# A mixture-of-experts block: how each expert tile gets its tokens and gate weights, when the expert outputs are fetched, and where the late sums stand

## The reference

```python
logits = flat_x @ Wr                                  # 4096 tokens, 8 experts
top_vals, top_idx = jax.lax.top_k(logits, 2)
rw = softmax(top_vals)                                # two weights per token
g = einsum('nc,ech->neh', flat_x, Wg)                 # C = 128, HIDDEN = 512
u = einsum('nc,ech->neh', flat_x, Wu)
h = silu(g) * u
eo = einsum('neh,ehc->nec', h, Wd) * DEPTH_SCALE
out = sum over the two chosen experts of rw * eo
x = x + attn_a(norm(x)); x = x + ffn(norm(x)); x = x + attn_b(norm(x)); x = x + ffn(norm(x))
```

## Time and profile before

| | us |
|---|---|
| median of three runs | 1116.42 (1113.54 to 1125.42) |
| profiled execution | 1122.49 |
| its span, first to last instruction | 1120.4 |
| PE / PEld busy in it | 1004.0 / 710.5 |
| DVE / ACT / POOL busy in it | 749.3 / 675.4 / 543.2 |

### The profile page before, as it was taken

How to read it: one execution, slowest core, us unless ns; L and a number is a source line. 1 busy time by engine, 2 the same in 40 slices (tenths; PEclk the granted TensorE clock), 3 DMA queues, 4 the chain that set the end, 5 groups by cost and what they waited for, 6 DMA issues and landing times.

```text
span 1120.4 us, 28587 instructions
## 1 busy us (share of the span) xinstructions
PE 1004.0 (90%) x9290; PEld 710.5 (63%) x9290; DVE 749.3 (67%) x2249; ACT 675.4 (60%) x1399; POOL 543.2 (48%) x764
## 2 busy tenths in 40 slices
PE   2999999999989999999798889999888899999990
PEld 1354555554568999999534444445544789999990
DVE  4697889877777333356778889998888753334542
ACT  2376777755644545555377779999778445455550
POOL 3143447634632710357776656588337155005465
PEclk9998999987989999999768889999889899999995
DMA  5444566534145977887743333343221578778973
GB/s 152 114 107 110 146 160 167 133 106 95 43 128 181 286 233 238 259 266 233 170 104 84 88 92 88 91 114 88 74 52 55 164 231 253 228 236 266 272 226 113
DMA packets 201721, 175.02 MB, mean 156 GB/s; under 512 B 19812, under 2 KB 160616, under 8 KB 201576
## 3 DMA queue, kind: packets, MB, share of 16 engines
q1 hardware_dynamic: 193384, 156.41, 50.6%
q0 software_dynamic: 8192, 16.79, 5.1%
HBM read 122.99 MB, written 50.14 MB: 155 GB/s over the span
## 4 chain that ended last, share of the span: by engine, by line
PE 61%; DVE 14%; SPq 8%; issue 6%; DMA 6%; POOL 3%; ACT 1%; POOLq 0%; DVEq 0%; ACTq 0%
PE psS L358 10%; PE psO L324 8%; PE psS L1399 7%; PE psT L1406 7%; DVE mx L664 5%; PE psS L389 4%; PE psN L1422 3%; PE psO L1422 3%; PE psM L279 3%; PE psN L331 3%; PE psT L366 2%; PE psM L429 2%; SPq L1476 2%; SPq L1471 2%; DMA xin<-xg 1%
## 5 line engine op out<-in xcount | busy, mean ns | idle before, releaser
L664 DVE TENSOR_REDUCE mx<-psS 128x3 f32<-128x384 f32 (+1 forms) x512 | 309.9, 618 | 88.7 <-PE psS L389 50.4
L358 PE MATMUL psS<-kst,qst 48*128 48x256 bf16 (+1 forms) x1024 | 195.8, 281 | 38.1 <-DVE mx L664 26.7
L561 ACT ACTIVATE pT<-psT,scb 128x512 f32<-128x512 f32 x256 | 192.5, 772 | 48.1 <-PE psT L366 46.0
L366 PE MATMUL psT<-qst,kst 50*128 50x256 bf16 (+1 forms) x1024 | 191.9, 274 | 4.1 <-DMA qst<-scr_m 1.8
L1463 DVE TENSOR_TENSOR hT<-sg,psT 128x512 f32<-128x512 f32 x142 | 97.5, 687 | 142.1 <-PE psT L1406 118.6
L1282 POOL DMA_INDIRECT xg<-xn,slot x128 | 123.2, 963 | 118.8 <-DVE ysb L1458 71.0
L1399 PE MATMUL psS<-xTt,wgc 128*128 128x128 f32 x1136 | 153.3, 278 | 3.7 <-issue 3.5
L556 ACT ACTIVATE pT<-psT 128x384 f32<-128x384 f32 x256 | 123.5, 489 | 54.8 <-PE psT L366 46.7
L1406 PE MATMUL psT<-xTt,wuc 128*128 128x128 f32 x1136 | 151.6, 277 | 1.1 <-DMA wuc<-in_L_ffn_Wu 1.1
L358 PEld LDWEIGHTS psS<-kst,qst 48*128 48x128 bf16 x1024 | 63.5, 96 | 138.1 <-DVE mx L664 71.6
L1296 POOL DMA_INDIRECT pT<-eo,slot x64 | 60.6, 947 | 175.3 <-DVE ysb L1458 105.5
(11 more groups left out here) (230 smaller groups left out, 1601.0 us busy)
## 6 DMA issues: line engine op xcount, KB each, us to landing
wgc<-in_L_ffn_Wg SPq DMA_DIRECT2D x142, 256.0 KB
wuc<-in_L_ffn_Wu SPq DMA_DIRECT2D x142, 256.0 KB
scr_part<-part SPq DMA_DIRECT2D x128, 128.0 KB, 2.1
qst<-scr_part SPq DMA_DIRECT2D x64, 192.0 KB, 3.7
kst<-scr_part SPq DMA_DIRECT2D x64, 192.0 KB, 4.6
xin<-xg SPq DMA_DIRECT2D x142, 64.0 KB
eo<-ysb SPq DMA_DIRECT2D x142, 64.0 KB
scr_part<-part SPq DMA_DIRECT2D x32, 192.0 KB, 1.9
```

The lines of the kernel that those rows point to most:

```text
L358: return nc.tensor.matmul(ps[:, c0:c0 + n], q_[r64, t, q0], k_[r64, t, 0:n], start=(half == 0), stop=True, skip_group_check=True)
L366: return nc.tensor.matmul(ps[:, c0:c0 + T - q0], k_[m64, t, half * P:half * P + P], q_[m64, t, q0:T], start=(half == 0 or not L.causal), s ...
L561: nc.scalar.activation(pT[:, g % 8, 0:cols], psT[g % 2][:, 0:cols], ACT.Exp, scale=scb[r][:, 0, i:i + 1], bias=scb[r][:, 1, i:i + 1]).then ...
L664: nc.vector.tensor_reduce(mx3[:, u, 0:n, pos:pos + 1].rearrange("p a b -> p (a b)"), psS[h % 2][:, 0:kcols(L)].rearrange("p (a k) -> p a k ...
```

## The change

1. **Tokens without PE and PSUM.** `xin` is now loaded in pairs of tiles (`tiles_of`: tile 0 alone, then 1 and 2, 3 and 4, ...) by four DMAs, one for each 32 features. Each lays 32x32 blocks side by side, in rows of 32 floats, which are 128 bytes. DVE transposes all blocks with one instruction per pair (`dve_columns`), straight into `xTt`. PE's transpose and ACT's copy are gone, and with them the waits for the PSUM bank `psM`.
2. **Gate weights resident.** `wg` (128 x 4096) is loaded in attention A, steps 4 to 11. `act_gate` copies the gate weights of tile k + 2 from it; SP's gate loads are gone.
3. **SP's order.** The up weights of tile k + 2 stand ahead of the token load, and the wait for the second group's scatters stands behind them.
4. **Fetches in three parts.** The second group's blocks are split at 9 and 13 (`PARTS`) instead of at 11: they need the tiles up to 57, 65 and 71. The tables cost a further comparison and table stage 8 is divided over k = 6 to 9. POOL's first-group fetches of the second expert stage are paced by `pair // 2` instead of `2 * pair // 3`. The last quad is added in two pieces (blocks 12; 13 to 15) and stored apart.
5. **Sums in halves.** In attention B the sums stand at heads 3 and 5 (step 6: 3 and 7) of steps 3, 4, 6 and 7, four additions each; POOL's fetches all stand at the end of its step. Some routing work of attention A moves by one or two heads.

```diff
-PART = 11
+PARTS = (9, 13)
-        xin = [sb(f"xin{i}", [P, D]) for i in range(FETCH)]
-        xTt = [sb(f"xTt{i}", [P, P]) for i in range(FETCH)]
+        xin = [sb(f"xin{i}", [P, 2 * D]) for i in range(2)]
+        xTt = [sb(f"xTt{i}", [P, 2 * P]) for i in range(2)]
...
             if k == ROUTE_LN:
                 dve.wait_ge((LA, LB)[l].s["x1"], NBLK)
+                dve_columns(dve, l, 0)
                 dve_ln_stats(dve, NBLK - 4, NBLK, s_ln[n])
+                dve_columns(dve, l, 1)
                 dve.wait_ge(s_ln[n], 2)
...
-            for pair in range(2 * PART if l == 1 else 0):
-                pool.wait_ge(f_sem["y"], n0 + TILES - 4 * PART // 3 + 2 * pair // 3)
+            for pair in range(2 * PARTS[1] if l == 1 else 0):
+                pool.wait_ge(f_sem["y"], n0 + OWN_A)
...
+        def act_gate(act, l, t):
...
+            chosen[n] = expert(act, l, t)
+            after(act, f_sem["g"], n - FETCH + 1)
+            nc.scalar.activation(wgc[n % FETCH][:], wg[:, bass.ds(chosen[n], HID)], ACT.Copy
+                                 ).then_inc(f_sem["wg"], 1)
...
+        def dve_columns(dve, l, m):
+
+            i, width = m % 2, P * len(tiles_of(m))
+            after(dve, f_ld[i], 64 * (PAIRS // 2 * l + m // 2 + 1))
+            after(dve, f_sem["u"], l * TILES + max(2 * m - 3, 0))
+            nc.vector.transpose(xTt[i][:, 0:width], xin[i][:, 0:width]).then_inc(f_sem["xT"], 1)
...
+        def sp_load(sp, l, m):
+
+            tiles = tiles_of(m)
+            rows = xg[tiles[0] * P:(tiles[-1] + 1) * P, :].rearrange("(t b) (f a) -> f b t a", b=SQ, a=SQ)
+            after(sp, f_sem["xT"], PAIRS * l + m - 1)
+            for f in range(D // SQ):
+                sp.dma_start(xin[m % 2][SQ * f:SQ * f + SQ, 0:P * len(tiles)].rearrange("b (t a) -> b t a", a=SQ),
+                             rows[f]).then_inc(f_ld[m % 2], 16)
...
-                if l == 1 and (j, h) in ((4, 9), (5, 9), (7, 2), (8, 4)):
-                    dve_combine_1(dve, 0, (4, 5, 7, 8).index(j))
+                if l == 1 and j in SUMS_AT and h in (3, 7 if j == 6 else 5):
+                    dve_combine_half(dve, 0, SUMS_AT.index(j), int(h > 3))
```

More of the change, by code:

```diff
@@ L1518, in sp_ffn @@
                     sp.wait_ge(r_gat[q], 16 * 8 * l)
-            for t in range(3):
-                sp_load(sp, l, t)
+            for m in range(2):
+                sp_load(sp, l, m)
             for k in range(TILES + 3):
@@ L1940, in _ @@
             pool_ffn(pool, 1)
-            for pair in range(2 * PART, 2 * SIZE[1]):
+            for pair in range(2 * PARTS[1], 2 * SIZE[1]):
                 pool_gather(pool, 3, pair)
```

245 lines of the change are left out of this document (128 added, 117 removed).

## The result

| | before | changed |
|---|---|---|
| median, us | 1114.98 (4 runs, 1113.12 to 1125.42) | 1102.70 (4 runs, 1096.30 to 1108.33) |
| ratio to before | 1 | 0.9876, 95% interval 0.9831 to 0.9921 |
| profiled execution / its span | 1122.49 / 1120.4 | 1101.90 / 1099.4 |
| 0 to tile 0 of expert stage 1 | 328.2 | 326.4 |
| stage 1, tile 0 to tile 70 | 209.7 | 210.8 |

The change gives 12 us by the medians and 21 between the two profiled spans; the forecast was 39.6. The 1102.7 lies just inside the stated range, 1062 to 1104, at the end where rival 2 stood and far from the forecast's 1077. The tail did what was forecast.

A forecast was written before the change was run, and what follows sets the result against it. It took PE to set the expert stages' pace at 2.79 us per tile, with DMA the second bound. Terms of -15.4 + 4.8 - 4.4 - 2.8 - 11 - 10.8 = -39.6 took 1116.4 to 1077 us; range 1062 to 1104.

The forecast's parts named there:

- rival 2: Expert stages: SP becomes the bound, token issues taking 0.8 us each, 2.86 us a tile, 1102 us; 6 in 100.
- SP as a cover: Expert stages: SP's issues take 4.5 us of a pair's 5.36, so they stay hidden behind PE.
- the other terms: Everything in the sum except PE's transpose: stage starts, routing, tile 23, attention B's sums and tail, together -24 us.
- PE's transpose, -15.4: Expert stages: without PE's transpose a tile takes 2.68 us, 0.11 less over 140 tile distances, -15.4 us.
- The covers ACT, DVE, DMA: Expert stages: per 2.68 us tile, ACT's 1.82 plus 0.4, DVE's 1.9 at most and DMA's 1.89 us stay hidden.
- Rival 1: Expert stages: small token packets make DMA the bound, at 78 ns each some 1230 us; 9 in 100.
- The start of the stages, +4.8: Start of both expert stages: DVE waits for four token loads before its norm statistics, +4.8 us, from +2 to +9.
- Routing, -4.4: Expert stages: spreading the expert table over four tiles removes tile 7's stall, 2.2 us each stage, -4.4, from -7 to 0.
- Tile 23, -2.8: Both expert stages: weights no longer stand behind the wait for the scatters, -2.8 us, from -5 to +1.
- Sums, -11: Attention B: sums in halves cut steps 4 to 8 from 104.1 to 93 us, -11, from -16 to 0.
- Rival 3: Attention B: halved sums don't help, PE still idles or they meet POOL; term 0, time 1088 us; 15 in 100.
- Tail, -10.8: After tile 70: POOL's second-group fetches start earlier and the last sum is a block shorter, -10.8 us, from -7 to -13.

The follow-up runs named there:

- b_act_store: The kernel before, with none of the change, but the tiles' result stores issued by ACT instead of SP: 1109.42 us, 0.9938 of before.
- as_sp_dummy: The changed kernel with stores issued by ACT, plus one unneeded 512-byte transfer per tile in SP's queue in their old place: 1100.20 us, 0.9864 of before.
- The single run: The changed kernel with stores issued by ACT and one part undone: attention B's sums (1090.52 us) or, for the tail, the first fetch part's end at block 11 (1097.84).

## Why the prediction was wrong, step by step

- **SP as a cover: the step that failed.** The prediction counted a pair at 4.5 us of 5.36, with two table reads "which I count as plain", 0.42 each. A read with the register instructions behind it takes 0.75 us (425.79 to 426.53), and the pair 5.13. The four token issues were priced right, 1.91 us for 1.96. So the margin was 0.2 us per pair, not 0.86, and the prediction had no term for irregular issues. The 18 long issues add 0.24 us to the average pair, so that SP needs as long as PE. Not every slow issue became a stall: after the one at 430.48 PE kept its pace. Together they and the missing room cost 15 to 16 us of the stages (409.6 and 410.5 us, against 394.3 with the stores on ACT) and 23 of the medians.
- **Rival 2 was the right one in its place.** It said that SP becomes the bound and the kernel takes 1102, and it was given 6 in 100. Its condition, 0.8 us per token issue and so an even 2.86 us per tile, was wrong: issues take 0.48 us on average, and quiet tiles keep 2.68 us between stalls. That its 1102 meets the 1102.7 is in part luck: it took the other terms at their full 24 us, and they gave less. The rival was argued away with the length of an issue ("issues in three dimensions took 0.49") where the length of a round had to be read. The trace of before had it: SP's rounds there take 2.5 to 2.65 us of 2.79, and `b_act_store` shows that 6 us hung on it even then. The Trainium skill (Perfetto Trace Analysis, What "DMA-bound" means) names an issuing engine whose track is solid with DMA slices as a limit of its own. Here the track was not solid, since nearly a third of a round (1.5 us of 5.13) were instructions that are no DMA slices. The same skill (Trainium Kernel Development and Optimization, Key Constraints) says that issuing from several engines saves only the issue time. Here that was worth 15 to 16 us of the stages, and `as_sp_dummy` agrees that it was time of the queue.
- **PE's transpose, -15.4.** Right where SP leaves room: quiet tiles take 2.68 us for 2.79. In the profile of the change most of it is eaten by the stalls.
- **The covers ACT, DVE, DMA.** They held. ACT has 13.45 us of 20 (forecast 13.5). DVE's transpose takes 445 ns for a pair. Of the 128-byte packets: between 425 and 450 us the rows below give 58.4% of 400 us of engine time, 233.6. By the packet records, 4096 packets of 128 bytes take 51.6 us of it, 12.6 ns each for the forecast 25; the other 544 of the 4640 have 4 bytes. Rival 1 needed 54 ns. The 39 ns for 512 bytes were misread: the window of the earlier trace rows also holds packets of 1 and 1.5 KB, and those of 512 bytes take 27.6 ns between 425 and 475 us of the kernel before. The Trainium skill's read-modify-write under 512 bytes (DMA: Bandwidth & Descriptors, Specifications), taken as double work, would be 78 ns with the prediction's price; the trace shows nothing like it for these loads.

```profile
DMA packets 6949, 3.53 MB, mean 141 GB/s; under 512 B 4640, under 2 KB 5793, under 8 KB 6945
...
q1 hardware_dynamic: 6945, 3.48, 58.4%
```

- **The start of the stages, +4.8.** Tile 0 to tile 3 takes 14.0 and 11.8 us with the stores on ACT, 11.5 and 10.0 in `b_act_store`: +4.3. Right in size, though in kernels with the same start the 14.0 and 11.8 read from 11.8 to 14.0 each.
- **Routing, -4.4: failed in size.** Above the pace, tiles 5 to 10 took 2.1 to 2.2 us in each stage of `b_act_store` and take 1.85 now: -0.6. The table's stall at tile 7 did go, and the added comparison built one at tile 5. The prediction had the comparison, "about 1 us of DVE", but did not add up DVE's whole tile: 5.1 us of routing in a row (341.74 to 346.87), of which PE's lead covers 3.5 (it waits 1.61). And part of the stalls that it counted as routing was SP's: these tiles of before were 3.2 and 4.2 us above the pace, and 2.1 each once the stores were on ACT.
- **Tile 23, -2.8.** -1.8 with SP free (tiles 23 to 26, both stages). In the changed kernel's stage 1 it is +1.9: tiles 24 and 25 take 4.68 and 5.46 us, 4.8 above the pace, where tiles 23 to 26 of before were 2.9 above it, since SP has no room to make up for the scatters' wait.
- **Sums, -11.** The single run gave 10.1 by the medians, and 7.1 in steps 3 to 8 of the profiles; the changed kernel's own profile gives 7.6 there. The prediction left step 3 out, which has a sum now. Steps 5 and 8 are at the undisturbed 16.7 us; step 6 was sized at 22.8 and took 24.7. Rival 3 (term 0) is excluded: without this part the kernel is 10.1 us slower, and the intervals do not meet.
- **Tail, -10.8.** -10.5 between the profiles, 9.9 in the single run.
- **The sum.** With SP free in both kernels the profiles differ by 1108.8 - 1078.1 = 30.7 us: stages -6.2 and -6.4, attention B -4.2, tail -11.8, ahead of tile 0 -2.2. What is missing to 39.6 is 3.8 us of routing, 1.0 of tile 23, 6.8 of attention B and 1 us of the stages that no term holds, less what the tail (1.0), the starts (0.5) and the part ahead of tile 0 (2.2) gave over. How much of the 6.8 the clock took is left open; it would take many profiles of each kernel to say.

## What to carry to other kernels

Before an issuing queue is called a cover, read the distance between two of the same rows a round apart in a stretch that does not wait, not the sum of its issues: reads of a table and other instructions without a row are in the one and not in the other. Then count the irregular issues in with the even ones, as an average per round. Here the even round filled 0.96 of its time, the irregular issues filled the rest, and freeing the queue was worth 15 us of the stages; before, at 0.90 to 0.95, it was worth 6 us in all. The view with the longest waits (59 us here) pointed at the buffer, and taking those waits away was worth nothing; what told cause from symptom was to put time back into the queue without the transfer that had held it. Such a run needs its own round read too: here it put back more than had been taken out.
